# Attention inner loop: the products with V gathered into two blocks per head, six slots of exponentials, maxima dealt 3, 5, 3, 5

## The chip, the cores and the metric

The kernel runs on one core of one Trainium2 chip. The core has five engines that run their own instruction streams and meet only at semaphores: TensorE (PE, whose weight loads are shown apart as PEld), VectorE (DVE), ScalarE (ACT), GpSimd (POOL) and SyncE (SP), which here only issues DMAs. The metric is the device time of one execution in microseconds. Before the change the median of 3 runs is 615.58 us (614.25 to 616.12).

## The reference

The program is one transformer layer on 1024 tokens (32 x 32) of 384 channels in float32: attention with 12 heads of 32 channels and a decomposed relative position bias, then a mixture of 8 experts. The change touches only the attention:

```
q, k, v = split(layernorm(x) @ w_qkv + b_qkv)          # 12 heads, 1024 x 32 each
attn = einsum('bnd,bmd->bnm', q * scale, k)             # 1024 x 1024 per head
attn = attn + rel_h[..., :, None] + rel_w[..., None, :]
attn = softmax(attn, axis=-1)
out  = attn @ v
x = x + out @ w_proj + b_proj
```

All of the expert part follows after that and is the same in both kernels.

## The kernel before, in words

For each head the bias is folded into the product: `qst` and `kst` hold 128 rows (q, its low part and the two bias factors against k and two one-hot rows), so that one 128-deep product gives scores with bias. The scores are made turned, with keys on partitions, so that the exponentials can be used as they are in the product with V.

A head takes these steps, and the work of several heads is interleaved on each engine.

- **Maxima** (PE `max_scores`, L536): for the row maximum, 16 matmuls of 128 x 512 per head make the scores once more with queries on partitions, alternately into PSUM banks 4 and 5. DVE takes the maximum of each (`reduce_max`, L1130). The matmul of piece p waits until the reduction of piece p - 2 is done. These are made one head ahead of the scores.
- **Turning the maxima**: DVE combines the halves (`whole_max`), PE transposes the 128 x 8 result (`turn_max`, L542), DVE negates it into `mneg` (`negate_max`), and SP copies it by DMA into a row of `qst` (`max_row`, L317). The first score matmul of the next head waits for that DMA (`mrow_in`).
- **Scores** (PE `scores`, L550): 8 tiles of 128 keys per head, 4 matmuls of 128 x 512 for each tile (two halves of the queries, two parts of the keys), into banks 0 and 1 for even tiles and 2 and 3 for odd ones. The first matmul of tile t waits until the exponential of tile t - 2 has emptied the banks.
- **Exponentials** (ACT, L924): one instruction of 128 x 1024 per tile, from PSUM into a slot of `prob`. There are 4 slots; a slot is free once PE has used it for V and, for the first 7 tiles, once POOL has added it to the sum.
- **Sum** (POOL `add_probs`, L390 and L394): POOL adds the exponentials of the first 7 tiles of a head into `acc`, 6 instructions of 128 x 1024.
- **Values** (PE `values`, L559): the product with V. `vh` (32 channels) is the stationary operand, and `quarters` spreads the 1024 queries over four column groups of the array, each 32 columns wide, so these matmuls use the array split into four tiles of 128 x 32, where all others use it whole. One call of `values` does a pair of score tiles, which the profile shows as 16 matmul records: four rounds of four that run side by side. With the last pair of a head come two more rounds for the sum of the last tile and two for `acc`.
- **Output** (ACT `copy_output` L929, PE `turn_output` L583, DVE `normalise`): the accumulated bank 6 is copied to `osb`, transposed into bank 7, and divided by the sum.

The order on PE is written out by hand in `head`. A head has four periods i = 0 to 3 of two score tiles each. Before the change each period begins with one call of `values` (pairs 2 and 3 of the head before, then pairs 0 and 1 of its own), followed by four maxima placed among the eight score matmuls: M ssss M ss M ss M (M for a maxima matmul, s for one of the scores). In period 2 `turn_output` follows the values, in period 3 `turn_max`. The four maxima of period 3 are already those of the head after next. The heads 1 to 9 run in a hardware loop of three heads per turn. Head 0 makes its 16 maxima in three periods (5, 5, 6), the last head makes none.

## Time and profile before

| | |
|---|---|
| median of 3 runs | 615.58 us (614.25 to 616.12) |
| the profiled execution, its own time | 615.08 us |
| its span | 613.3 us |
| mean granted TensorE clock | 0.996 |
| attention loop in the trace | about 82 to 289 us |

The page gives for each engine its busy time and what it waited for. A matmul's record lasts from its start to a modelled end, and records overlap, since the next begins before the last has drained; the distance from start to start is what a matmul costs. A row of the timeline gives the start, the time from there to the end of the last instruction merged into it, the engine, the line of the code, the tiles written and read, and the number of instructions. Behind it, in brackets, stands idle time of the engine and what ended it.

### The profile page before, as it was taken

The numbers are of one execution on the slowest core, as the hardware profiler recorded it, in microseconds if no ns is written. First come the engines' busy times: TensorE is split into PE (matmuls) and PEld (weight loads), VectorE is DVE, ScalarE is ACT, GpSimd is POOL, SyncE is SP. The second block draws the span as 40 slices with busy tenths as digits, with TensorE's granted clock in tenths as the row PEclk, the third lists the DMA queues.
The fourth block names the chain that finished last, engine by engine and source line by source line (L and its number), as shares of the span: only waits on it lengthen the run. The fifth ranks groups of instructions, "written<-read, shape, count | busy, mean of one in ns | idle before, by whom it ended". The sixth has DMA issues, their size and how long they took to land.

```text
span 613.3 us, 11388 instructions
## 1 busy us (share of the span) xinstructions
PE 590.4 (96%) x4409; PEld 501.9 (82%) x4409; DVE 386.7 (63%) x644; ACT 297.8 (49%) x411; POOL 195.1 (32%) x114
## 2 busy tenths in 40 slices
PE   2998999999999999999998999999999999999996
PEld 2886876666666666666997999999999999999994
DVE  6557767676767666642789875555476545477535
ACT  3555425454545454455456534444555444355523
POOL 0400047898888888898300000000000000000000
PEclk9999999999999999999989999999999999999999
DMA  8046054332344444102050624444442444542302
GB/s 272 7 87 129 3 117 98 69 64 60 68 86 86 86 86 86 40 2 88 17 192 4 228 84 152 153 154 155 155 152 82 156 154 155 155 155 82 113 1 103
DMA packets 37414, 63.39 MB, mean 103 GB/s; under 512 B 3864, under 2 KB 32894, under 8 KB 37246
## 3 DMA queue, kind: packets, MB, share of 16 engines
q1 hardware_dynamic: 37374, 62.83, 36.3%
q8 instruction: 29, 0.48, 0.3%
q14 instruction: 11, 0.09, 0.0%
HBM read 44.16 MB, written 1.57 MB: 75 GB/s over the span
## 4 chain that ended last, share of the span: by engine, by line
PE 91%; DVE 4%; ACT 1%; DMA 1%; SPq 1%; issue 1%; DVEq 0%
PE ps L767 21%; PE ps L783 21%; PE ps L550 14%; PE ps L559 10%; PE ps L536 8%; PE ps L460 8%; DVE rhalf L1130 2%; PE ps L490 1%; PE ps L445 1%; PE ps L701 1%; PE ps L583 1%; DMA onehot<-c_onehot 1%; PE ps L738 1%; PE ps L794 1%; PE ps L713 1%; DVE xs L1296 1%
## 5 line engine op out<-in xcount | busy, mean ns | idle before, releaser
L1130 DVE TENSOR_REDUCE rhalf<-ps 128x1 f32<-128x512 f32 x192 | 131.2, 690 | 40.7 <-PE ps L536 39.8
L924 ACT ACTIVATE prob<-ps 128x1024 f32<-128x1024 f32 x96 | 98.0, 1026 | 97.0 <-PE ps L550 87.5
L394 POOL TENSOR_TENSOR acc<-acc,prob 128x1024 f32<-128x1024 f32 x58 | 139.6, 2406 | 5.9 <-POOL acc L390 0.8
L550 PE MATMUL ps<-qst,kst 128*128 128x512 f32 x384 | 110.6, 394 | 0.0
L767 PE MATMUL ps<-xeh,wih 128*128 128x320 f32 x288 | 89.6, 311 | 1.0 <-ACT xeh L986 1.0
L421 POOL CAST dpc<-dpt 120x1024 fp32r<-120x1024 f32 (+1 forms) x3 | 3.1, 1037 | 273.4 <-PE ps L803 216.6
L783 PE MATMUL ps<-hh,woh 128*128 128x320 f32 x288 | 89.2, 310 | 0.0
L783 PE MATMUL ps<-hh,wol 128*128 128x320 f32 x288 | 89.0, 309 | 0.0
L767 PE MATMUL ps<-xeh,wil 128*128 128x320 f32 x288 | 89.0, 309 | 0.0
L783 PE MATMUL ps<-hl,woh 128*128 128x320 f32 x288 | 89.0, 309 | 0.0
L767 PE MATMUL ps<-xel,wih 128*128 128x320 f32 x288 | 89.0, 309 | 0.0
L550 PEld LDWEIGHTS ps<-qst,kst 128*128 128x128 f32 x384 | 71.8, 188 | 15.2 <-issue 0.8
L536 PE MATMUL ps<-kst,qst 128*128 128x512 f32 x192 | 80.6, 423 | 2.4 <-DVE rhalf L1130 1.3
L1207 DVE TENSOR_TENSOR wol<-raw_o,woh 128x1152 fp32r<-128x1152 f32 x32 | 43.4, 1356 | 50.8 <-ACT woh L959 50.8
L990 ACT ACTIVATE hh<-ps 128x320 fp32r<-128x320 f32 x96 | 41.7, 439 | 55.8 <-PE ps L767 55.0
L959 ACT ACTIVATE woh<-raw_o 128x1152 fp32r<-128x1152 f32 x32 | 37.4, 1168 | 50.0 <-PE ps L783 50.0
L1202 DVE TENSOR_TENSOR wil<-raw_i,wih 128x1152 fp32r<-128x1152 f32 x32 | 43.4, 1357 | 24.4 <-ACT wih L954 24.4
L1281 DVE SCALAR_TENSOR_TENSOR hl<-ps,hh 128x320 fp32r<-128x320 f32 x96 | 45.9, 488 | 19.9 <-ACT hh L990 17.7
L767 PEld LDWEIGHTS ps<-xeh,wih 128*128 128x128 f32 x288 | 54.1, 188 | 1.2 <-ACT xeh L986 1.2
L767 PEld LDWEIGHTS ps<-xel,wih 128*128 128x128 f32 x288 | 54.1, 188 | 0.0
L783 PEld LDWEIGHTS ps<-hl,woh 128*128 128x128 f32 x288 | 54.1, 188 | 0.0
L783 PEld LDWEIGHTS ps<-hh,woh 128*128 128x128 f32 x288 | 54.1, 188 | 0.0
(159 smaller groups left out, 876.3 us busy)
## 6 DMA issues: line engine op xcount, KB each, us to landing
raw_i<-in_L_ffn_wi SPq DMA_DIRECT2D x32, 576.0 KB, 5.1
raw_o<-in_L_ffn_wo SPq DMA_DIRECT2D x32, 576.0 KB, 4.1
xs<-in_x SPq DMA_DIRECT2D x8, 384.0 KB, 4.7
qst<-qh SPq DMA_DIRECT2D x12, 256.0 KB, 3.2
qst<-relh SPq DMA_DIRECT2D x12, 256.0 KB, 3.8
qst<-relw SPq DMA_DIRECT2D x12, 256.0 KB, 4.4
kst<-kp SPq DMA_DIRECT2D x12, 256.0 KB, 5.0
qst<-ql SPq DMA_DIRECT2D x12, 128.0 KB, 3.1
```

Source lines behind the costliest of these rows:

```text
L394: nc.gpsimd.tensor_tensor(acc[:, :], acc[:, :], prob[:, t % SLOT, :], ALU.add).then_inc(sum_add, 1)
L460: done = mm(out_bank, a, b, start=first and n == 0, stop=last and n == 2)
L536: mm(bank(4 + half), qst[b][:, 0, t * P:(t + 1) * P], kst[b][:, 0, half * BANK:(half + 1) * BANK], start=True, stop=True).then_inc(max_mm, 1)
L550: last = mm(bank(2 * (t % 2) + half), kst[b][:, part, t * P:(t + 1) * P], qst[b][:, part, half * BANK:(half + 1) * BANK], start=part == 0, ...
L559: last = mm(bank(6)[HD * j:HD * (j + 1), cols], stationary, moving[:, j * Q4:(j + 1) * Q4], start=start, stop=stop, skip_group_check=True)
L767: last = mm(bank(k, SLOTS), w[:, b, c, k * P:(k + 1) * P], xe[:, c, e, :], start=c == 0 and n == 0, stop=c == DC - 1 and n == 2)
L783: last = mm(bank(3 + c, SLOTS), w[:, b, k, c * P:(c + 1) * P], h[:, b, k, :], start=s == 0 and k == 0 and n == 0, stop=s == UNITS - 1 and ...
L924: run(prob[:, t % SLOT, :], ps[:, 2 * (t % 2) * BANK:2 * (t % 2 + 1) * BANK], ACT.Exp).then_inc(exp_done, 1)
L1130: ve.tensor_reduce(rhalf[:, p // 2, p % 2:p % 2 + 1], bank(4 + p % 2), AX_X, ALU.max).then_inc(max_red, 1)
L1202: ve.tensor_tensor(wil[:, b, :, :], raw_i[:, b, :, :], wih[:, b, :, :].bitcast(F32), ALU.subtract).then_inc(wi_lo, 1)
L1207: ve.tensor_tensor(wol[:, b, :, :], raw_o[:, b, :, :], woh[:, b, :, :].bitcast(F32), ALU.subtract).then_inc(wo_lo, 1)
L1281: stt(out=hl[:, b, k, :], in0=bank(k, SLOTS), scalar=0.0, in1=hh[:, b, k, :].bitcast(F32), op0=ALU.max, op1=ALU.subtract).then_inc(h_lo, 1)
```

## The change

The change is in the attention loop and has these parts.

- PE: the four pairs of a head are no longer dealt one to each period. Pairs 2 and 3 of the head before (with the sum) stand together ahead of period 1, pairs 0 and 1 together ahead of period 3. Periods 0 and 2 begin with scores.
- PE: the maxima are dealt 3, 5, 3, 5 to the periods, in place of four each. A period of five has the pattern M ss M ss M ss M ss M, one of three ssss M ss M ss M.
- `turn_max` writes into bank 5 (before, bank 7), and the second maxima matmul of the head after next, which also writes bank 5, waits for `mneg_ready`. `turn_output` moves to period 3, directly behind `turn_max`.
- ACT and POOL: `prob` has 6 slots, tile t of head h sits in slot (8 h + t) mod 6. The waits in `free_slot` follow from that. ACT's loop now has three heads per turn.
- DVE: `normalise` of a head comes one head later, ahead of the ninth maximum. Near the end `normalise(NH - 3)` and `normalise(NH - 2)` stand around `attn_low(1)`.
- `mneg` and `bpj` are placed elsewhere in SBUF, to make room.

The core of the diff:

```
-    SLOT = 4
+    SLOT = 6
...
+        def slot_of(j, t):
+            return (NT * j + t) % SLOT
...
+                if p == 1:
+                    wait(pe, mneg_ready, h)
...
             def turn_max(h):
                 pe.wait_ge(max_whole, h + 1)
-                wait(pe, o_normed, h - 1)
-                nc.tensor.transpose(bank(7)[0:NT, 0:P], rmax[:, :], ident[:, :]).then_inc(max_turned, 1)
+                nc.tensor.transpose(bank(5)[0:NT, 0:P], rmax[:, :], ident[:, :]).then_inc(max_turned, 1)
...
+            PIECES = [(5, 8), (8, 13), (13, 16)]
+            NEXT = PIECES[0][0]
...
-                        pieces = [(after, p) for p in range(4)] if more else []
+                        pieces = [(after, p) for p in range(NEXT)] if more else []
...
-                        pieces = [(nxt, p) for p in range(4 * i + 4, 4 * i + 8)]
-                    if i > 1:
-                        values(h, b, i - 2)
-                    elif not first:
-                        values(h - 1, (b - 1) % 3, i + 2)
-                    if i == 2 and not first:
-                        wait(pe, mneg_ready, h + 1)
-                        turn_output(h - 1)
-                    if i == 3 and not last:
-                        turn_max(h + 1)
-                    maxima(pieces[0:1])
+                        pieces = [(nxt, p) for p in range(*PIECES[i])]
+                    if i == 1 and not first:
+                        values(h - 1, (b - 1) % 3, 2)
+                        values(h - 1, (b - 1) % 3, 3)
+                    if i == 3:
+                        values(h, b, 0)
+                        values(h, b, 1)
+                        if last:
+                            pe.wait_ge(o_normed, NH - 2)
+                        else:
+                            turn_max(h + 1)
+                        if not first:
+                            turn_output(h - 1)
+                    ahead = int(len(pieces) > HALF)
+                    maxima(pieces[0:ahead])
                     scores(h, b, 2 * i, 0)
+                    maxima(pieces[ahead:2 * ahead])
                     scores(h, b, 2 * i, 1)
-                    maxima(pieces[1:2])
+                    maxima(pieces[2 * ahead:2 * ahead + 1])
                     scores(h, b, 2 * i + 1, 0)
-                    maxima(pieces[2:3])
+                    maxima(pieces[2 * ahead + 1:2 * ahead + 2])
                     scores(h, b, 2 * i + 1, 1)
-                    maxima(pieces[3:])
+                    maxima(pieces[2 * ahead + 2:])
...
             def free_slot(h, t):
-                if t % 2 == 0:
-                    wait(act, pv_mm, PAIRS_T * h + t // 2 - 1)
-                if t < ADDED - SLOT:
-                    wait(act, sum_add, (ADDED - 1) * h + t - (ADDED - 1 - SLOT))
-                elif t >= SLOT:
-                    wait(act, sum_add, (ADDED - 1) * h + max(1, t - SLOT))
+                then, was = (h, t - SLOT) if t >= SLOT else (h - 1, t + NT - SLOT)
+                if was % 2 == 0:
+                    wait(act, pv_mm, PAIRS_T * then + was // 2 + 1)
+                if was < ADDED:
+                    wait(act, sum_add, (ADDED - 1) * then + max(1, was))
```

How the order moves on PE is shown at head 10, the first behind the loop, where no register instructions stand between. The place is the start of its period 0. L536 makes maxima, L550 scores, L559 values (`vh_101` is V of head 9). Before:

```order
L559 MATMUL ps<-prob,vh_101 32x256 [waits exp_done]
L559 MATMUL ps<-prob,vh_101 32x256 x7
L536 MATMUL ps<-kst_95,qst_92 128x512 [waits max_red]
L550 MATMUL ps<-qst_91,kst_94 128x512 [waits exp_done,mrow_in]
L550 MATMUL ps<-qst_91,kst_94 128x512 x3
L536 MATMUL ps<-kst_95,qst_92 128x512 [waits max_red]
L550 MATMUL ps<-qst_91,kst_94 128x512 [waits exp_done]
L550 MATMUL ps<-qst_91,kst_94 128x512
L536 MATMUL ps<-kst_95,qst_92 128x512 [waits max_red]
L550 MATMUL ps<-qst_91,kst_94 128x512 x2
L536 MATMUL ps<-kst_95,qst_92 128x512 [waits max_red]
L559 MATMUL ps<-prob,vh_101 32x256 [waits exp_done]
```

The same place after the change, where the lines are L557 for scores, L544 for maxima and L566 for values:

```order
L557 MATMUL ps<-qst_90,kst_93 128x512 [waits exp_done,mrow_in]
L557 MATMUL ps<-qst_90,kst_93 128x512 x3
L544 MATMUL ps<-kst_94,qst_91 128x512 [waits max_red]
L557 MATMUL ps<-qst_90,kst_93 128x512 [waits exp_done]
L557 MATMUL ps<-qst_90,kst_93 128x512
L544 MATMUL ps<-kst_94,qst_91 128x512 [waits max_red]
L557 MATMUL ps<-qst_90,kst_93 128x512 x2
L544 MATMUL ps<-kst_94,qst_91 128x512 [waits max_red]
L566 MATMUL ps<-prob,vh_100 32x256 [waits exp_done]
L566 MATMUL ps<-prob,vh_100 32x256 x7
L566 MATMUL ps<-prob,vh_100 32x256 [waits exp_done]
L566 MATMUL ps<-prob,vh_100 32x256 x7
```

The values that opened the period are gone from there, with one maxima matmul, and stand with the next pair at its end. The scores of a head now begin directly behind those of the head before.

The second place is where head 10 ends and head 11 begins, which has no maxima. Before (L542 is `turn_max`):

```order
L542 MATMUL ps<-ident,rmax 8x128 [waits o_normed,max_whole]
L550 MATMUL ps<-qst_91,kst_94 128x512 [waits exp_done]
L550 MATMUL ps<-qst_91,kst_94 128x512 x3
L550 MATMUL ps<-qst_91,kst_94 128x512 [waits exp_done]
L550 MATMUL ps<-qst_91,kst_94 128x512 x3
L559 MATMUL ps<-prob,vh_102 32x256 [waits exp_done]
L559 MATMUL ps<-prob,vh_102 32x256 x7
L550 MATMUL ps<-qst_92,kst_95 128x512 [waits exp_done,mrow_in]
L550 MATMUL ps<-qst_92,kst_95 128x512 x3
L550 MATMUL ps<-qst_92,kst_95 128x512 [waits exp_done]
L550 MATMUL ps<-qst_92,kst_95 128x512 x3
```

After (L549 is `turn_max`, L590 `turn_output`):

```order
L549 MATMUL ps<-ident,rmax 8x128 [waits max_whole]
L590 MATMUL ps<-ident,osb 128x128 [waits o_copied]
L590 MATMUL ps<-ident,osb 128x128 x3
L557 MATMUL ps<-qst_90,kst_93 128x512 [waits exp_done]
L557 MATMUL ps<-qst_90,kst_93 128x512 x3
L557 MATMUL ps<-qst_90,kst_93 128x512 [waits exp_done]
L557 MATMUL ps<-qst_90,kst_93 128x512 x3
L557 MATMUL ps<-qst_91,kst_94 128x512 [waits exp_done,mrow_in]
L557 MATMUL ps<-qst_91,kst_94 128x512 x3
L557 MATMUL ps<-qst_91,kst_94 128x512 [waits exp_done]
L557 MATMUL ps<-qst_91,kst_94 128x512 x3
```

Four tiles of scores, 16 matmuls, now follow one another with nothing between.

## Rows read from the trace of the kernel before

**Rows 1.** The page, busy time of each engine.
```profile
PE 590.4 (96%) x4409; PEld 501.9 (82%) x4409; DVE 386.7 (63%) x644; ACT 297.8 (49%) x411; POOL 195.1 (32%) x114
```

**Rows 2.** Critical chain, 98 to 262 us: start, duration, what.
```profile
102.93 1.86 PE ps L559 x32
...
258.44 1.86 PE ps L559 x32
```

**Rows 3.** Groups by line, 122.2 to 139.4 us.
```profile
L1130 DVE TENSOR_REDUCE rhalf<-ps 128x1 f32<-128x512 f32 x16 | 11.0, 691 | 3.8 <-PE ps L536 3.7
...
L924 ACT ACTIVATE prob<-ps 128x1024 f32<-128x1024 f32 x8 | 8.2, 1025 | 7.4 <-PE ps L550 7.2 <-POOL acc L394 0.3
...
L550 PEld LDWEIGHTS ps<-qst,kst 128*128 128x128 f32 x32 | 6.0, 188 | 1.2
```

**Rows 4.** Timeline of PE, 131.5 to 148.5 us.
```profile
132.74 0.62 PE L550 MATMUL ps<-qst,kst 128*128 128x512 f32 x2
133.20 0.39 PE L536 MATMUL ps<-kst,qst 128*128 128x512 f32 x1
133.52 1.07 PE L559 MATMUL ps<-prob,vh 128*32 128x256 f32 x16
134.52 0.50 PE L536 MATMUL ps<-kst,qst 128*128 128x512 f32 x1
134.85 1.09 PE L550 MATMUL ps<-qst,kst 128*128 128x512 f32 x4
...
137.15 0.40 PE L536 MATMUL ps<-kst,qst 128*128 128x512 f32 x1
...
139.34 0.50 PE L536 MATMUL ps<-kst,qst 128*128 128x512 f32 x1
...
145.86 0.63 PE L550 MATMUL ps<-qst,kst 128*128 128x512 f32 x2
146.32 0.40 PE L536 MATMUL ps<-kst,qst 128*128 128x512 f32 x1
146.65 1.07 PE L559 MATMUL ps<-prob,vh 128*32 128x256 f32 x16
147.71 0.27 PE L542 MATMUL ps<-ident,rmax 128*8 128x128 f32 x1
```

**Rows 5.** Timeline of DVE, 131.5 to 149.5 us.
```profile
147.49 0.17 DVE L1134 TENSOR_REDUCE rmax<-rhalf 128x8 f32<-128x16 f32 x1
```

**Rows 6.** Timeline of PE in head 0, 82 to 98.5 us.
```profile
84.78 0.98 PE L536 MATMUL ps<-kst,qst 128*128 128x512 f32 x2
85.97 0.50 PE L536 MATMUL ps<-kst,qst 128*128 128x512 f32 x1 [0.20 <-DVE rhalf L1130]
```

**Rows 7.** Timeline of ACT, 131.5 to 149.5 us and 260 to 292 us.
```profile
133.47 1.02 ACT L924 ACTIVATE prob<-ps 128x1024 f32<-128x1024 f32 x1 [0.26 <-PE ps L550]
136.14 1.03 ACT L924 ACTIVATE prob<-ps 128x1024 f32<-128x1024 f32 x1 [1.64 <-PE ps L550]
...
146.52 1.02 ACT L924 ACTIVATE prob<-ps 128x1024 f32<-128x1024 f32 x1 [0.21 <-PE ps L550]
...
270.01 1.94 ACT L924 ACTIVATE prob<-ps 128x1024 f32<-128x1024 f32 x2 [1.55 <-PE ps L550]
```

**Rows 8.** Timeline of POOL, 258 to 292 us.
```profile
260.49 2.40 POOL L390 TENSOR_TENSOR acc<-prob 128x1024 f32<-128x1024 f32 x1 [2.21 <-PE ps L559]
263.04 12.49 POOL L394 TENSOR_TENSOR acc<-acc,prob 128x1024 f32<-128x1024 f32 x5
```

**Rows 9.** Waits, 98 to 262 us: total, times, longest.
```profile
ACT prob L924 <- POOL acc L394: 9.5, 6, 1.9
```

**Rows 10.** Timeline of SP from 130 us; DMA share, 131.0 to 133.4 us in 40 slices.
```profile
131.12 0.70 SPq L317 DMA_DIRECT2D qst<-mneg  x1
...
DMA  0000000000000000000000002100000000000000
```

**Rows 11.** Busy time of the engines and granted clock by stretch.
```profile
315.00:325.00 10.00, 8.41 (x54) 7.75 (x53) 8.48 (x44) 4.36 (x6) 0.00 (x0) 0.84 0.22 61
```

More of the change, by code:

```diff
@@ L96, in metaformer_layer @@
     wqkl, wvl = place("wqkl", [P, DC, 2 * D], F32R, u3), place("wvl", [P, DC, D], F32R, v3)
-    SLOT = 4
+    SLOT = 6
     prob = place("prob", [P, SLOT, T], F32, u2)
     acc = place("acc", [P, T], F32, u2 + 4 * SLOT * T)
-    assert 4 * (SLOT + 1) * T <= TD + 4 * DC * 2 * D
     bv = new("bv", [P, D])
-    bpj = new("bpj", [P, D])
+    at[0] = max(at[0], u2 + 4 * (SLOT + 1) * T)
     qh, ql = (new(n, [P, DC, T], F32R) for n in ("qh", "ql"))
@@ L121, in metaformer_layer @@
     vh = [new(f"vh{b}", [P, NT, HD]) for b in range(3)]
-    mneg = new("mneg", [NT, P], F32R)
+    mneg = place("mneg", [NT, P], F32R, o4 + 7 * BANK)
     rl = new("rl", [P, 2, NT // 2])
@@ L128, in metaformer_layer @@
     b6 = place("b6", [2 * DC, P], F32, o4 + 6 * BANK)
+    bpj = new("bpj", [P, D])
     top = at[0]
@@ L384, in head_values, with add_probs @@
                 nc.gpsimd.tensor_copy(vh[b][:, :, :], vt[:, :, bass.ts(h, HD)]).then_inc(vh_ready, 1)
-            def add_probs(h, added=ADDED):
+            def add_probs(h, j, added=ADDED):
                 pool.wait_ge(exp_done, NT * h + 2)
                 wait(pool, pv_mm, PAIRS_T * h)
-                nc.gpsimd.tensor_tensor(acc[:, :], prob[:, 0, :], prob[:, 1, :], ALU.add).then_inc(sum_add, 1)
+                nc.gpsimd.tensor_tensor(acc[:, :], prob[:, slot_of(j, 0), :], prob[:, slot_of(j, 1), :], ALU.add).then_inc(sum_add, 1)
                 for t in range(2, added):
@@ L393, in add_probs @@
                     pool.wait_ge(sum_add, (ADDED - 1) * h + t - 1)
-                    nc.gpsimd.tensor_tensor(acc[:, :], acc[:, :], prob[:, t % SLOT, :], ALU.add).then_inc(sum_add, 1)
+                    nc.gpsimd.tensor_tensor(acc[:, :], acc[:, :], prob[:, slot_of(j, t), :], ALU.add).then_inc(sum_add, 1)
             head_values(0, 0)
@@ L400, in _ @@
             head_values(1, 1)
-            add_probs(0)
+            add_probs(0, 0)
             with pool.Fori(0, (NH - 3) // 3) as i:
@@ L568, in values @@
                 for t in (2 * i, 2 * i + 1):
-                    last = quarters(slice(0, Q4), vh[b][:, t, :], prob[:, t % SLOT, :], t == 0, t == NT - 1)
+                    last = quarters(slice(0, Q4), vh[b][:, t, :], prob[:, slot_of(b, t), :], t == 0, t == NT - 1)
                 if i == PAIRS_T - 2 and h_last:
@@ L572, in values @@
                     for t in range(LAST_ADDED, NT - 1):
-                        last = quarters(slice(Q4, 2 * Q4), ones[:, 0:HD], prob[:, t % SLOT, :], False, False)
+                        last = quarters(slice(Q4, 2 * Q4), ones[:, 0:HD], prob[:, slot_of(b, t), :], False, False)
                 if i == PAIRS_T - 1:
-                    quarters(slice(Q4, 2 * Q4), ones[:, 0:HD], prob[:, (NT - 1) % SLOT, :], False, False)
+                    quarters(slice(Q4, 2 * Q4), ones[:, 0:HD], prob[:, slot_of(b, NT - 1), :], False, False)
                     pe.wait_ge(sum_add, (ADDED - 1) * (h + 1) - (ADDED - LAST_ADDED) * h_last)
@@ L681, in _ @@
             project(0, (0, 1))
+            pe.wait_ge(o_normed, NH - 1)
             turn_output(NH - 1)
@@ L923, in exps @@
                     free_slot(h, t)
-                    run(prob[:, t % SLOT, :], ps[:, 2 * (t % 2) * BANK:2 * (t % 2 + 1) * BANK], ACT.Exp).then_inc(exp_done, 1)
+                    run(prob[:, slot_of(j, t), :], ps[:, 2 * (t % 2) * BANK:2 * (t % 2 + 1) * BANK], ACT.Exp).then_inc(exp_done, 1)
                     between(t)
@@ L934, in attn_high @@
                     run(ath[:, c, half * BANK:(half + 1) * BANK], bank(4 + half), ACT.Copy).then_inc(turn_act, 1)
-            exps(0, lambda t: None)
-            with act.Fori(1, NH - 1) as h:
-                exps(h, lambda t: copy_output(h - 1) if t == 1 else None)
+            exps(0, 0, lambda t: None)
+            with act.Fori(0, (NH - 3) // 3) as i:
+                for j in range(1, 4):
+                    exps(3 * i + j, j % 3, lambda t: copy_output(3 * i + j - 1) if t == 1 else None)
+            exps(NH - 2, (NH - 2) % 3, lambda t: copy_output(NH - 3) if t == 1 else None)
             def last_between(t):
@@ L1150, in normalise, with head @@
                                  rl[:, :, :].unsqueeze(3).broadcast_to([P, 2, HALF, HD]), ALU.mult).then_inc(o_normed, 1)
-            def head(h, first=False, more=True):
-                for p in range(0 if first else 4, 2 * NT):
-                    if p == 12 and not first:
-                        normalise(h - 1)
+            NEXT = 5
+            def head(h, first=False, early=False, more=True):
+                for p in range(0 if first else NEXT, 2 * NT):
+                    if p == 8 and not first and not early:
+                        normalise(h - 2)
                     reduce_max(h + 1, p)
+                if not first and not early:
+                    dve.wait_ge(o_normed, h - 1)
                 whole_max(h + 1)
@@ L1160, in head @@
                 if more:
-                    for p in range(4):
+                    for p in range(NEXT):
                         reduce_max(h + 2, p)
@@ L1174, in _ @@
             head(0, first=True)
-            with dve.Fori(1, NH - 2) as h:
+            head(1, early=True)
+            with dve.Fori(2, NH - 2) as h:
                 head(h)
@@ L1187, in _ @@
             ve.tensor_tensor(wpl[:, :, :], wpj[:, :, :], wph[:, :, :].bitcast(F32), ALU.subtract).then_inc(wp_lo, 1)
+            normalise(NH - 3)
+            attn_low(1)
             normalise(NH - 2)
-            attn_low(1)
             normalise(NH - 1)
```

12 lines of the change are left out of this document (6 added, 6 removed).

## The prediction, on record before the changed kernel ran

> **What bounds the kernel now.** I read the page's busy times first: PE is busy 96% of the span and DVE, the next, 63% [rows 1]. Then the chain of waits over the attention loop: it consists of PE work, and the long values blocks, one per head, give the head's period. The first and the last of ten such blocks start at 102.93 and 258.44 us, so nine heads take 155.51 us, 17.28 us each [rows 2]. In one head DVE reduces for 11.0 us and ACT makes exponentials for 8.2 us [rows 3]; POOL adds for 2.40 + 12.49 us, from 260.49 to 275.53 [rows 8]. All have slack, so in this loop only what lies on PE counts.
>
> Then the timeline of PE, from start to start. Two scores and the maxima matmul behind them go from 145.86 to 146.32, 0.23 us for each [rows 4]. The 48 matmuls of a head thus take about 11.0 of the 17.28 us. A short values block goes from 133.52 to 134.52, and from the maxima matmul ahead of it to the one behind it 1.32 us pass (133.20 to 134.52). For the long block, eight rounds in place of four, it is 2.19 us (137.15 to 139.34) [rows 4]. So a round costs (2.19 - 1.32) / 4 = 0.22 us, and the first matmul behind a block takes 0.33 us to the next (134.52 to 134.85) in place of 0.23. What a block costs beyond its rounds is therefore 1.32 - 4 x 0.22 - 0.23 + 0.10 = 0.32 us (with 0.217 for a round). That is the price of leaving the 128 x 128 form of the array for the 128 x 32 form and coming back, and it is what this change is about.
>
> **The change part by part.**
>
> *Blocks.* Before, head 0 has 2 blocks of values, heads 1 to 10 have 4 each, head 11 has 5 (the last two pairs are one block): 47. After, they are 1, 20 and 3: 24. The rounds stay the same. 23 x 0.32 = -7.4 us, all on PE's path.
>
> *`turn_max`.* It now comes behind two pairs of values. Before, PE waits for DVE there: the combined maximum ends at 147.49 + 0.17 = 147.66 [rows 5] and the transpose starts at 147.71, 1.06 us after its block began, where the unhindered block takes 1.00 [rows 4]. With a block one us longer that wait is gone: 11 x 0.06 = -0.6 us. Its flag reaches PE 0.05 us after DVE's end, which I use below.
>
> *Maxima 3, 5, 3, 5.* The pattern M ss keeps 3 x 0.23 = 0.69 us between maxima, and a reduction takes 0.691 [rows 3]. Five in a row are no tighter than four. In head 0 the maxima are not covered: at the end of a period two stand together and then the next period's one, at 84.78, some 0.5 later and 85.97 [rows 6], the last after idle time on DVE. Three adjacent ones take 85.97 - 84.78 = 1.19 us from the first to the third in place of 0.46, so 0.7 too much. By the order this place and two like it cost about 1.8 us in all (0.7, 0.3 for a pair, 0.7). The new order has three pairs, at 0.3 to 0.4 each, 1.0. So -0.8 us (0 to -1.2).
>
> *Waits of scores for exponentials.* This is the price. Two pairs of banks hold the scores; a block between the periods gave ACT time. Now periods 3 and 0, and 1 and 2, touch. Let x be the start of the last score matmul of a tile. The exponential starts at x + 0.43 if nothing else precedes it (x = 145.86 + 0.23, exponential at 146.52), at x + 0.50 (132.74 + 0.23, 133.47) or at x + 0.59 (134.85 + 3 x 0.23, 136.14) where ACT first passes one or two waits against a register [rows 4, 7]. It takes 1.03, and the flag 0.05. Then PE must load: 0.10 us if only the exposed part counts (the 0.33 against 0.23 behind a block), 0.19 if the whole load does [rows 3]. Of an odd tile (7, 3) the next tile but one should start seven matmuls later, x + 1.61 (one maxima, four scores, one maxima): it can at x + 1.61 to 1.70 for tile 7 and at x + 1.68 to 1.77 for tile 3, going by the waits that ACT's order has there. For the even tiles (6, 2) eight matmuls lie between, x + 1.84 against 1.77 to 1.86. Sum per head 0.07 to 0.27 us; an exponential that starts a little late adds to it. I take 0.2, near the upper end, since the load of a waiting matmul beside a running one shows as 188 ns [rows 3]. Ten heads: +2.0 us (0.7 to 3.4).
>
> The Trainium skill, page "TensorE: Matmul & The Clock Gate", section "LDWEIGHTS (loading the stationary operand)", gives columns / 1.2 in ns, 107 ns for 128 columns. By that rule these waits would cost near their lower end, some 0.7 us, and the sum would be 608.3. The trace has both numbers, 0.10 exposed and 188 ns for a load beside a matmul [rows 3, 4], and no wait of this kind.
>
> *Scores without maxima.* From period 3 of head 10 to period 0 of head 11, and in periods 1 and 2 of head 11, four tiles follow each other without any maxima. There the next tile but one is due five matmuls after x, at 1.15, but the exponential allows 0.43 + 1.03 + 0.05 + 0.10 to 0.19 = 1.61 to 1.70: about 0.5 us. The tile after that is bound to the second of two exponentials, which end 1.94 after the first began [rows 7]: about 0.1. Twice this is +1.3 us (0.8 to 1.7). Before, a block of values covered it.
>
> *What costs nothing, and its cover.* The DMA of the maxima row: SP issues at 131.12, 0.6 us after the transpose, and its packets move at 132.5 [rows 10], 2.0 us after the transpose. The score that needs it comes behind `turn_output` and thirteen matmuls, some 3.6 us after it (before 4.35). SP's queue is otherwise the same. POOL's sum: the chain of one head runs from 0.6 us after the last read of `acc` for 15.0 us [rows 8], and PE wants the result about 16.3 us after that read: 0.7 us of cover. The longer ACT loop and the later `normalise` lie on engines with slack. ACT's waits for slots, 9.5 us in ten heads [rows 9], go away with six slots, but no PE matmul waited at their end, so that gives nothing.
>
> *Sum.* -7.4 - 0.6 - 0.8 + 2.0 + 1.3 = -5.5 us. The profiled execution took 615.08 us, so 609.6; it lies 0.5 below the median of the runs, and between 609.6 and 610.1 I say 609.8.
>
> **The rivals.**
>
> *A. The waits for exponentials don't show.* For it: with the exposed load alone most of them are within 0.1 us of being met. Then -8.8 + 0.7 + 0.8 = -7.3, 607.8, and with waits fully absorbed 606.5. Against: tile 3 is late by either count.
>
> *B. The waits are as large as the gain.* If ACT starts every exponential at x + 0.59 and loads count in full, the odd tiles are late by 0.25 and the even ones by 0.03, and ACT falls behind by 0.1 at each: 0.7 us per head, the worth of two blocks and the turn wait (2 x 0.32 + 0.06). Only head 0 and head 11 remain: 614.5, no change.
>
> *C. Slower: the two pairs of score banks become the bound.* Place: tiles 0, 1, 4 and 5 of each head. It decides from 0.18 us at each of the four places. Each wait delays the next exponential, so that ACT and PE take turns rather than overlap; at 0.3 us each it is +1.2 per head against -0.7, and the kernel takes 615.1 + 5 - 1 = 619. Against it: ACT is idle 7.4 us in each head [rows 3] and catches up in every block.
>
> *D. The adder.* POOL's chain of 15.6 us with the read of `acc` behind it binds only if PE's head gets below 16.2 us. I expect 16.8. In rival A the head takes 16.6 us, so even there it does not bind, and it cannot make the kernel slower; it has no chance of its own here.
>
> *E. The clock.* From 315 to 325 us the mean granted clock is 0.84 [rows 11], that is a stretch of 3.2 us at 1.2 GHz (0.16 x 10 x 2) in the routing, while PE had little to do. Work before it now ends 5 us earlier, and the low stretch may fall on matmuls that count. Half of it, 1.6 us, would be lost at most, and 0.5 won at best.
>
> **How the numbers follow.** The forecast with its own range, 606.9 to 612.3 (every wait at its bounds), has 0.70. A has 0.14. B, with anything between 612.3 and 615, has 0.11. C has 0.04 and E carries 0.01 past the edge. The range 606.5 to 613.6 takes A and E's loss, and a part of B. What a measurement of this kernel can tell from no change is about 0.3%, 1.85 us: faster means below 613.7. That is the forecast, A and a small part of B, 0.85; same 0.11; slower 0.04.
>
> **What would show it.** The chain's long blocks, twelve rounds now, should repeat every 16.8 us (16.5 to 17.0) in place of 17.28. PE's timeline should show two blocks per head, one with values x32 then the sum's 16 records, one with values x32, `turn_max` and `turn_output`, and the same 1.00 us and 0.33 at the edges. Waits of scores for ACT should appear at the first matmul of tiles 1 and 5, 0.0 to 0.3 us each, and about 0.5 us at tile 0 of head 11 and at its tile 4. ACT should no longer wait for POOL. The prediction is wrong if a block of four tiles costs more than 8 x 0.22 + 0.32, if the waits exceed 0.35 us per head, or if PE waits for POOL's sum or for the maxima row.

## The result and the profile after

| | us |
|---|---|
| changed kernel, 4 runs | 608.72 median (608.3 to 610.03) |
| kernel before, 4 runs on the same chip | 615.12 median (614.25 to 616.12) |
| ratio | 0.9895, 95% interval 0.9877 to 0.9914 |
| the changed kernel's profiled execution | 610.03, span 608.2, mean granted clock 0.994 |

The kernel is 1.05% faster, 6.4 us by the medians; 609.8 had been forecast, within 606.5 to 613.6. The profiled execution is the slowest of the four, and the trace says why (below, at the clock).

The chain of waits of the changed kernel, 98 to 270 us (start, duration, what), still consists of PE work. The long blocks, now twelve rounds:

```profile
100.69 2.73 PE ps L566 x48
...
117.26 2.73 PE ps L566 x48
...
133.83 2.73 PE ps L566 x48
...
150.72 2.73 PE ps L566 x48
...
167.32 2.73 PE ps L566 x48
```

They repeat every 16.57 to 16.60 us where it was 17.28 [rows 2], except from 133.83 to 150.72, which is 16.89. I return to that one.

PE's timeline of the same kernel, 131.5 to 150.5 us, is to be read from start to start:

```profile
133.44 0.40 PE L544 MATMUL ps<-kst,qst 128*128 128x512 f32 x1
133.76 1.93 PE L566 MATMUL ps<-prob,vh 128*32 128x256 f32 x32
135.51 0.61 PE L566 MATMUL ps<-prob,ones 128*32 128x256 f32 x8
135.95 0.61 PE L566 MATMUL ps<-acc,ones 128*32 128x256 f32 x8
136.49 0.50 PE L544 MATMUL ps<-kst,qst 128*128 128x512 f32 x1
136.83 0.63 PE L557 MATMUL ps<-qst,kst 128*128 128x512 f32 x2
...
140.53 0.39 PE L544 MATMUL ps<-kst,qst 128*128 128x512 f32 x1
140.75 0.70 PE L557 MATMUL ps<-qst,kst 128*128 128x512 f32 x2
141.30 0.39 PE L544 MATMUL ps<-kst,qst 128*128 128x512 f32 x1
...
142.31 1.93 PE L566 MATMUL ps<-prob,vh 128*32 128x256 f32 x32
144.17 0.27 PE L549 MATMUL ps<-ident,rmax 128*8 128x128 f32 x1
...
147.49 0.40 PE L544 MATMUL ps<-kst,qst 128*128 128x512 f32 x1
147.90 1.20 PE L557 MATMUL ps<-qst,kst 128*128 128x512 f32 x4
148.94 0.40 PE L544 MATMUL ps<-kst,qst 128*128 128x512 f32 x1
```

Three things are to be seen. The price of a block is as before: from the maxima matmul ahead of the long block to the one behind it 3.05 us pass (133.44 to 136.49), and 3.05 - 12 x 0.217 - 0.23 + 0.11 = 0.33 us. The one visible stop of a head is at tile 5: two scores from 140.75 to 141.30, 0.55 in place of 0.46 [rows 4]. And at 147.49, where the loop of three heads turns, PE needs 0.41 us to the next score and 1.04 us for the four scores of the tile, against 0.23 and 0.91 elsewhere: 0.31 us once in three heads.

What was waited for, 98 to 262 us (total, times, longest):

```profile
...
POOL acc L400 <- ACT prob L938: 4.6, 9, 0.8
PEld ps L557 <- ACT prob L938: 4.3, 19, 0.4
```

The 4.3 us in 19 waits are 17 weight loads at tiles 1 and 5 and two directly behind a turn of the loop (0.42 and 0.39 us). At the tiles nearly all of it is time in which PE still worked on the matmul before. ACT's wait for POOL [rows 9] is gone, and nothing on PE waits for the maxima row or for POOL's sum.

To compare runs I cut every trace at four points of PE's timeline: the first maxima matmul behind the values' projection, the first read of `acc`, the tenth read of `acc`, and the first matmul of the output's projection. These give head 0 and most of head 1, nine heads of the loop, and the tail. For the changed kernel the ends are these rows:

```profile
82.34 0.39 PE L544 MATMUL ps<-kst,qst 128*128 128x512 f32 x1
...
102.81 0.61 PE L566 MATMUL ps<-acc,ones 128*32 128x256 f32 x8
...
282.76 0.44 PE L466 MATMUL ps<-wph,ath 128*128 128x384 f32 x1
```

All traces together ("low" is the time at 1.2 GHz behind the attention, without the last 0.7 to 2.3 us of the program, which are at 1.2 GHz in every trace):

| kernel | heads 0-1 | nine heads | tail | attention | from there to the end | low |
|---|---|---|---|---|---|---|
| before | 21.93 | 155.52 | 29.76 | 207.21 | 323.77 | 3.4 |
| changed | 20.47 | 149.85 | 30.10 | 200.42 | 325.38 | 6.8 |
| changed, again | 20.44 | 150.00 | 30.13 | 200.56 | 323.76 | 3.4 |
| four blocks | 21.84 | 154.75 | 29.85 | 206.43 | 324.74 | 3.4 |
| four slots | 20.61 | 149.92 | 30.30 | 200.83 | 323.36 | 0 |
| split blocks | 21.62 | 156.03 | 29.97 | 207.61 | 325.18 | 6.8 |
| maxima 4, 4, 4, 4 | 20.37 | 149.05 | 30.18 | 199.61 | 325.23 | 6.8 |
| maxima between | 20.41 | 149.46 | 30.13 | 199.99 | 323.74 | 3.4 |
| turn at a block | 20.41 | 149.60 | 30.14 | 200.14 | 325.19 | 6.8 |
| three edits | 20.41 | 148.91 | 29.52 | 198.84 | 323.72 | 3.4 |
| three edits, again | 20.42 | 148.94 | 29.49 | 198.85 | 325.19 | 6.8 |
| three edits, 4444 | 20.36 | 148.84 | 29.47 | 198.68 | 325.23 | 6.8 |
| three edits, four slots | 20.57 | 148.98 | 29.69 | 199.25 | 323.78 | 3.4 |

The attention repeats to 0.15 us between executions of one kernel, the rest only to 1.6, and the last column goes with it but for one trace (324.74). So the sum is checked against the attention, where the change is: -6.79 us.

### The profile page after: what moved, and what is told of

Its sections match the earlier page's. It is cut to its first block, busy times and chain, and to the rows that moved or that the text cites. A ratio compares the mean times of both kernels' runs of the same rounds, so it can differ in the third digit from the quotient of the medians.

```text
span 608.2 us, 11363 instructions
## 1 busy us (share of the span) xinstructions
PE 584.4 (96%) x4409; PEld 504.5 (83%) x4409; DVE 387.2 (64%) x644; ACT 297.9 (49%) x411; POOL 195.3 (32%) x114
## 4 chain that ended last, share of the span: by engine, by line
PE 90%; DVE 5%; ACT 2%; DMA 1%; issue 1%; SPq 1%; DVEq 0%
PE ps L782 21%; PE ps L798 21%; PE ps L557 14%; PE ps L566 9%; PE ps L466 8%; PE ps L544 7%; DVE rhalf L1146 2%; PE ps L716 1%; PE ps L496 1%; PE ps L451 1%; DMA onehot<-c_onehot 1%; PE ps L753 1%; PE ps L728 1%; PE ps L809 1%; PE ps L590 1%
## 5 line engine op out<-in xcount | busy, mean ns | idle before, releaser
L557 PE MATMUL ps<-qst,kst 128*128 128x512 f32 x384 | 115.6, 397 | 0.9 <-ACT prob L938 0.9
L557 PEld LDWEIGHTS ps<-qst,kst 128*128 128x128 f32 x384 | 70.0, 188 | 19.2 <-ACT prob L938 5.5
L544 PE MATMUL ps<-kst,qst 128*128 128x512 f32 x192 | 78.4, 412 | 2.0 <-DVE rhalf L1146 0.9
```

Source lines behind the costliest of these rows:

```text
L544: mm(bank(4 + half), qst[b][:, 0, t * P:(t + 1) * P], kst[b][:, 0, half * BANK:(half + 1) * BANK], start=True, stop=True).then_inc(max_mm, 1)
L557: last = mm(bank(2 * (t % 2) + half), kst[b][:, part, t * P:(t + 1) * P], qst[b][:, part, half * BANK:(half + 1) * BANK], start=part == 0, ...
```

## The experiments

My theory: the gain is the number of blocks, 0.32 us each, less small waits of scores for exponentials. Rivals: the gain comes from the other edits (slots, bank, the deal of maxima), or the waits cost as much as foreseen and the blocks are worth more.

**Four blocks.** The changed kernel, with the values and maxima in the order of before:

```diff
-            PIECES = [(5, 8), (8, 13), (13, 16)]
+            PIECES = [(4, 8), (8, 12), (12, 16)]
...
-                    if i == 1 and not first:
-                        values(h - 1, (b - 1) % 3, 2)
-                        values(h - 1, (b - 1) % 3, 3)
+                    if i > 1:
+                        values(h, b, i - 2)
+                    elif not first:
+                        values(h - 1, (b - 1) % 3, i + 2)
...
+                    cut = [pieces[0:1], [], pieces[1:2], pieces[2:3], pieces[3:]]
...
```

> The changed kernel with one part undone: the pairs of values are dealt one to each period again and the maxima 4 to a period in the old pattern (M ssss M ss M ss M); six slots, bank 5 for the turned maxima and turn_output behind turn_max stay. Theory (the gain is the form changes of the array): back to about 614 to 615 us, head period 17.2 us (17.28 less the 0.06 that turn_max no longer waits in a few heads, if that), ACT's waits for POOL gone all the same. Rival (the gain comes from the free slots or from the bank of the turned maxima): stays at 609 to 611.

Measured: 614.14 us (613.71 to 616.12, 10 runs), ratio to before 0.9985 (0.9969 to 1.0001). The attention is 0.78 us shorter than before; a head takes 17.19 us. The bank, the slots, the place of `turn_output` and the later `normalise` are worth 0.8 us together, the regrouping (with its deal of maxima and with the turn wait) 6.0. The turn wait is not in the 0.8, for in this kernel it is still there. PE's timeline, 144.5 to 147.8 us:

```profile
145.54 1.07 PE L566 MATMUL ps<-prob,vh 128*32 128x256 f32 x16
146.60 0.27 PE L549 MATMUL ps<-ident,rmax 128*8 128x128 f32 x1
```

The transpose starts 1.06 us behind its block's start, as before [rows 4], at ten of the eleven places (1.13 at the last), and each time 0.05 us behind the end of DVE's combined maximum. Of the 0.8 us, 0.3 is a delay that the kernel before has in the first head of each turn of the loop: at 113.11, 165.00 and 216.84 us the maxima matmul behind `turn_max` starts 0.19 us after it, in the other heads 0.09. With four blocks it is gone. The rest is 0.05 us a head, of which 0.03 lie where `turn_output` now stands right behind `turn_max`. The cause of the delay was not looked for.

**Four slots.** One number of the changed kernel:

```diff
-    SLOT = 6
+    SLOT = 4
```

> The changed kernel with SLOT = 4. Theory: slots alone gave nothing before, but with blocks of four tiles the exponentials of tiles 0 and 1 cannot start until the block has read their slots, and the scores of tiles 2 and 3 behind the block wait for them: about 1.3 to 1.6 us more at each of two blocks, head period 19 to 20 us, 640 to 650 us in all. Rival (the slots don't matter, ACT has 7 us of idle time in a head): 609.

Measured: 607.57 us (606.44 to 609.6, 4 runs), ratio 0.988 (0.9849 to 0.9912); attention 200.83. I was wrong by over 30 us: the slots are not needed, and in the attention they are worth 0.4 us. ACT's timeline of this kernel, 131 to 138 us, shows it:

```profile
134.30 1.94 ACT L938 ACTIVATE prob<-ps 128x1024 f32<-128x1024 f32 x2 [2.86 <-PE ps L566]
136.12 0.60 ACT L943 ACTIVATE osb<-ps 128x512 f32<-128x512 f32 x1
137.65 1.03 ACT L938 ACTIVATE prob<-ps 128x1024 f32<-128x1024 f32 x1 [0.92 <-PE ps L557]
```

and PE's:

```profile
133.08 1.93 PE L566 MATMUL ps<-prob,vh 128*32 128x256 f32 x32
...
135.81 0.50 PE L544 MATMUL ps<-kst,qst 128*128 128x512 f32 x1
136.15 0.62 PE L557 MATMUL ps<-qst,kst 128*128 128x512 f32 x2
```

A block of two pairs gives back the slots of its first pair after four rounds, so the exponentials of tiles 0 and 1 run from 134.30 to 136.24, beside the rest of the block (the four rounds of its first pair end about 0.9 us behind 133.08). Tile 2 wants the first one's banks at 136.15, when it has been done (at 135.3) for 0.8 us. What I had overlooked is that the two exponentials that wait have a whole block as cover.

**Split blocks.** The changed kernel, with the first maxima matmul of a period moved from behind the block in between its two calls of `values`, so that a head has four blocks again while the scores stand as in the changed kernel:

```diff
-                    for head_max, p in pieces:
+                    for head_max, p in filter(None, pieces):
...
                         values(h - 1, (b - 1) % 3, 2)
+                        maxima(pieces[0:1])
+                        pieces = [None] + pieces[1:] if pieces else []
                         values(h - 1, (b - 1) % 3, 3)
                     if i == 3:
                         values(h, b, 0)
+                        maxima(pieces[0:1])
+                        pieces = [None] + pieces[1:] if pieces else []
                         values(h, b, 1)
```

> The changed kernel with one maxima matmul moved from behind each block into its middle, so that the array changes form twice more per head, 20 more blocks in heads 0 to 10; the matmuls are the same. Theory (0.32 us for each block beyond its rounds): +6.4 us, 615 us, head period 17.2 us. Rival (blocks cost their rounds only, the gain came with what else moved, the dealing of maxima and the turn waits): 609.

Measured: 615.96 us (614.93 to 617.21, 10 runs), ratio 1.0008 (0.9992 to 1.0024). Attention 207.61, +7.19 us against the changed kernel for 20 more blocks: 0.36 us each. In the nine heads alone it is +6.18 us for 18 blocks, 0.34 each. PE's timeline of this kernel, 116 to 136 us:

```profile
117.82 0.39 PE L544 MATMUL ps<-kst,qst 128*128 128x512 f32 x1
118.14 1.07 PE L566 MATMUL ps<-prob,vh 128*32 128x256 f32 x16
119.14 0.49 PE L544 MATMUL ps<-kst,qst 128*128 128x512 f32 x1
119.56 1.07 PE L566 MATMUL ps<-prob,vh 128*32 128x256 f32 x16
120.45 0.61 PE L566 MATMUL ps<-prob,ones 128*32 128x256 f32 x8
120.88 0.61 PE L566 MATMUL ps<-acc,ones 128*32 128x256 f32 x8
121.42 0.73 PE L557 MATMUL ps<-qst,kst 128*128 128x512 f32 x2
```

One single maxima matmul inside the block costs 1.42 us from block start to block start (118.14 to 119.56) where its four rounds take 0.87 and the matmul 0.23: 0.32 us more. The matmuls are the same in both kernels, so this settles that leaving the 128 x 32 form and coming back is what was paid for; what the array does in that time no run shows. The gain of the whole change is undone by it (207.61 against 207.21 us before), so no other part of it carries the gain: the rest comes to nothing on balance.

**Maxima 4, 4, 4, 4.** The changed kernel, with four maxima in each period, one ahead of each two scores (M ss M ss M ss M ss):

```diff
-            PIECES = [(5, 8), (8, 13), (13, 16)]
+            PIECES = [(4, 8), (8, 12), (12, 16)]
...
-                    ahead = int(len(pieces) > HALF)
-                    maxima(pieces[0:ahead])
+                    cut = [pieces[0:1], pieces[1:2], pieces[2:3], pieces[3:4], pieces[4:]]
+                    maxima(cut[0])
                     scores(h, b, 2 * i, 0)
-                    maxima(pieces[ahead:2 * ahead])
+                    maxima(cut[1])
...
```

> The changed kernel with its two blocks, but the maxima dealt 4 to each period as M ss M ss M ss M ss. Theory: the only waits of scores for exponentials in a full head are 0.10 us at tile 5 and 0.0 to 0.03 at tile 1, where four scores stand together; with a maxima matmul between all pairs these tiles start eight matmuls after the tile before and never wait: head period 16.47 in place of 16.57, -1.0 us. Rival (the dealing 3, 5, 3, 5 is itself needed, since DVE cannot take sixteen maxima at 0.69 us without the gaps): PE waits for DVE, 16.6 us or more.

Measured: 608.29 us (606.87 to 609.68, 6 runs), ratio 0.9883 (0.9859 to 0.9908). Attention 199.61, 0.81 us less than with 3, 5, 3, 5. PE's timeline of this kernel, first ahead of a block of values, then where the loop turns (between the scores at 147.24 and the maxima matmul at 147.69):

```profile
133.25 0.40 PE L544 MATMUL ps<-kst,qst 128*128 128x512 f32 x1
133.48 0.62 PE L557 MATMUL ps<-qst,kst 128*128 128x512 f32 x2
134.03 1.93 PE L566 MATMUL ps<-prob,vh 128*32 128x256 f32 x32
...
147.24 0.62 PE L557 MATMUL ps<-qst,kst 128*128 128x512 f32 x2
147.69 0.39 PE L544 MATMUL ps<-kst,qst 128*128 128x512 f32 x1
147.92 0.61 PE L557 MATMUL ps<-qst,kst 128*128 128x512 f32 x2
```

At tiles 1 and 5 hardly a stop is left, the heads take 16.52 to 16.60 us, and the turn's 0.3 us is gone: 147.24 to 147.69 and 147.69 to 147.92 are the pace. A head without a turn still gains only 0.03 of the 0.1 expected. The block's entry is not what takes it back: 0.55 us behind the start of two scores (133.48 to 134.03) is 0.09 more than the pace of 0.46, the same 0.09 as 0.32 against 0.23 behind a maxima matmul. What takes part of it back is the pace itself: the 44 intervals of a head between such matmuls are 231.8 ns in the mean, stops of over 15 ns left out, where they are 230.7 in the changed kernel, 0.05 us a head. Why was not tested. The deal of 3 and 5 is therefore no part of the gain: it costs 0.8 us, most of it at the loop's turns.

**Turn at a block.** The end of PE's loop moved from ahead of period 0 to ahead of period 1:

```diff
-            def head(h, n, b, first=False, last=False, more=True):
+            def head(h, n, b, first=False, last=False, more=True, periods=range(4)):
...
-                for i in range(PAIRS_T):
+                for i in periods:
...
-                    head(3 * i + j, i + j // 3, j % 3)
+                    head(3 * i + j, i + j // 3, j % 3, periods=range(1, 4))
+                    head(3 * i + j + 1, i + (j + 1) // 3, (j + 1) % 3, periods=range(1))
```

> The changed kernel, with the end of the three-head loop moved on every engine: the loop body now holds periods 1, 2, 3 of a head and period 0 of the next, so PE's jump stands just ahead of the block of values of periods 1, not ahead of four scores. Theory (the jump costs about 0.3 us where scores follow it directly, because their weight loads cannot be fetched ahead, and less where a block follows, whose mode change is paid anyway): the two heads with a turn take 16.6 to 16.7 us in place of 16.89 and 16.84, the others stay at 16.57 to 16.60, the loop over nine heads 149.4 in place of 149.85. Rival (the 0.3 us is the maxima or another wait that happens to fall in that head): the turns still take 16.85, or the cost moves to another head whole. Time 608.2 to 608.7 either way.

In this text "on every engine" says too much: only PE's loop is cut differently, the loops of the others are as they were. Measured: 607.73 us (606.93 and 608.52), ratio 0.9874 (0.9847 to 0.9901). All nine heads take 16.59 to 16.66 us: no turn stands out any more, the others are 0.03 longer, and the nine heads take 149.60, -0.25. PE's timeline of this kernel at its turn:

```profile
149.16 0.39 PE L544 MATMUL ps<-kst,qst 128*128 128x512 f32 x1
149.47 1.93 PE L566 MATMUL ps<-prob,vh 128*32 128x256 f32 x32
```

0.31 us from a maxima matmul to a block, as at every other block (0.32). So the 0.3 us belonged to the jump with scores directly behind it; a wait for maxima would have stayed where it was. A block behind the jump hides it, and with 4, 4, 4, 4 a single maxima matmul behind the jump does too. Why the scores pay and the others don't is not shown: the text's reason, that their weight loads cannot be fetched ahead, was not tested.

**Maxima between.** Only the places of the maxima in a period of three changed:

```diff
-                    ahead = int(len(pieces) > HALF)
-                    maxima(pieces[0:ahead])
+                    cut = [pieces[k:k + 1] for k in range(4)] + [pieces[4:]] if len(pieces) > HALF else [[]] + [pieces[k:k + 1] for k in range(3)] + [pieces[3:]]
+                    maxima(cut[0])
                     scores(h, b, 2 * i, 0)
-                    maxima(pieces[ahead:2 * ahead])
+                    maxima(cut[1])
...
```

> The changed kernel, with the maxima inside a period dealt otherwise: a period of three has two scores ahead of each maxima matmul (ss M ss M ss M ss), one of five stays M ss M ss M ss M ss M. Theory (the stop of 0.08 to 0.095 us at tiles 1 and 5 comes from how early the first score of the tile stands behind the previous tile's exponential; two scores later for the maxima changes which tile is early): the head period goes from 16.57 to 16.47 us, the nine heads from 149.85 to about 149. Rival (the head is bound by DVE's reductions of 0.69 us, so an equal pitch moves the stop and doesn't remove it): 16.55 to 16.60. Attention as a whole 199.4 to 200.5 us.

Measured, one run: 606.24 us. A head takes 16.55 us, the turns still 16.82, the nine heads 149.46: -0.39 where I expected about -0.9. The rival's figure was nearer, but not its reason: PE does not stop for DVE. The stops at tiles 1 and 5 are gone, and as with 4, 4, 4, 4 the pace of the other matmuls is 1 ns longer (231.6 ns).

**Three edits.** Both of these and, in the last head, the values by single pairs:

```diff
-                    if i == 1 and not first:
+                    if last and i < 2:
+                        values(h - 1, (b - 1) % 3, i + 2)
+                    elif i == 1 and not first:
...
+                    if last and i == 2:
+                        values(h, b, 0)
                     if i == 3:
-                        values(h, b, 0)
+                        if not last:
+                            values(h, b, 0)
                         values(h, b, 1)
...
```

> Three edits on the changed kernel together: maxima ss M ss M ss M ss in the periods of three, the loop's end ahead of the block of values, and in the last head the values dealt one tile at a time (two blocks more, 0.64 us, against 1.3 us of waits of scores for exponentials, so -0.6). Theory: period 16.47 to 16.55, turns within 0.1 of it, the tail from the last acc read of the loop to the first projection matmul 29.4 to 29.6 in place of 30.10; attention 198.5 in place of 200.42, time 606.7. Rival (the waits of the tail only move to the other blocks): tail 30.1 to 30.7, attention 199.5 to 200.

Measured: 606.82 us (604.5 to 607.61, 5 runs), ratio 0.9856 (0.9832 to 0.9881). Attention 198.84, tail 29.52. The last head of the changed kernel and of this one, from PE's timelines; first the changed:

```profile
261.28 2.07 PE L557 MATMUL ps<-qst,kst 128*128 128x512 f32 x8
263.65 2.08 PE L557 MATMUL ps<-qst,kst 128*128 128x512 f32 x8 [0.30 <-ACT prob L938]
...
269.26 2.11 PE L557 MATMUL ps<-qst,kst 128*128 128x512 f32 x8
271.94 2.12 PE L557 MATMUL ps<-qst,kst 128*128 128x512 f32 x8 [0.57 <-ACT prob L938]
```

and with the three edits:

```profile
259.08 2.09 PE L557 MATMUL ps<-qst,kst 128*128 128x512 f32 x8
261.11 1.07 PE L566 MATMUL ps<-prob,vh 128*32 128x256 f32 x16
262.11 2.11 PE L557 MATMUL ps<-qst,kst 128*128 128x512 f32 x8
```

Eight scores take 8 x 0.23 = 1.84 us; in the changed kernel the next eight follow 2.37 and 2.68 us behind, 0.53 and 0.84 late. A single block in between costs its own 0.32 and covers that. The tail is 0.58 shorter; 0.6 had been expected.

**Three edits with 4, 4, 4, 4.**

> As the kernel with all three edits, but with four maxima in each period (M ss, four times) in place of three and five: period 16.52 to 16.60 as measured for four and four alone, no cost at the turn, the tail 29.4 to 29.6: attention 199.0 us, time 607.0 to 607.5. If the deal of the maxima matters for the waits, this one and the one with three and five differ by over 0.05 us per head; if only the number of blocks does, they are equal.

Measured: 607.74 us (607.54 to 608.86, 4 runs), ratio 0.9873 (0.9854 to 0.9893); attention 198.68, nine heads 148.84 against 148.91. By the rule in the text the two are equal, so the deal no longer matters once the turn and the place of the maxima are right. Their medians are 0.9 us apart; in the traces the difference lies behind the attention (323.72 and 325.23 us).

**Side by side.** The changed kernel, the three edits, and the three edits with four slots, on one chip:

> The changed kernel once more, as the yardstick for the two others of this call: 608.3 to 608.9 us by the runs so far, attention 200.4 us in the trace.

> The kernel with three edits on the changed one (maxima of the periods of three behind two scores each, loop's end ahead of a block, the last head's values one tile pair at a time), once more beside the changed kernel. Theory: the attention stretch is 1.5 us shorter again (198.8 to 200.4) and the medians differ by as much, 606.9 against 608.5. Rival: the gain is given back behind the attention, where the granted clock falls for a stretch or two of 3.4 us whenever work moves, so the medians differ by under 0.8 us.

> The same with four slots of exponentials in place of six. Theory, from the run of the changed kernel with four slots (loop 149.92 against 149.85): the slots give nothing, so attention 198.8 to 199.3 us and the same median as with six. Rival: the tighter order leaves ACT too little room with four slots, attention over 200 us.

Measured: 609.2 us (608.22 to 611.42), 607.74 (606.71 to 608.1) and 607.78 (606.46 to 609.24), 6 runs each; before 615.63. The attention takes 200.56, 198.85 and 199.25 us. The three edits beat the changed kernel by 1.7 us in the attention and 1.5 by the medians, and the traces of the pair even have the low stretches the other way round. The intervals of their ratios to before, 0.9867 (0.9838 to 0.9896) and 0.9898 (0.9867 to 0.993), overlap, so by time alone the difference is likely rather than sure; in the trace it has now repeated. The medians also compare unlike executions: all six of the three edits had a mean granted clock of 0.993, of the changed kernel's only two, and these two took 611.42 and 609.76 us against 606.71 to 608.1. Of the expectations the first missed (609.2 against 608.3 to 608.9), the second has the difference right, and the third has the slots right: 0.4 us, no more, the same as without the three edits.

## Why the prediction was right, point by point

**Blocks, -7.4.** Right. The price of 0.32 us was read from two blocks [rows 4]; the split costs 0.36 each over 20 blocks, 0.34 over the 18 of the nine heads, 0.32 in the rows of one.

**`turn_max`, -0.6.** Right, by the rows. In the changed kernel the transpose starts 1.86 us behind its block's start (142.31 to 144.17), which is eight rounds and the 0.12 that an unhindered block shows too (1.00 against 0.87), and DVE's combined maximum ended at 143.31, 0.86 us earlier. The experiment with four blocks does not show it, since the wait is still in it.

**Maxima in head 0, -0.8.** Right in size, wrong in its name. Heads 0 and 1 take 1.46 us less, of which two blocks are 0.64. With four blocks they gain 0.09, with 4, 4, 4, 4 they gain 1.56. So the 0.8 comes, as far as these orders part it, from the place between the first tile's two pairs of scores, which was empty before and in the kernel with four blocks, and is used with 3, 5, 3, 5 and with 4, 4, 4, 4. The deal 3, 5, 3, 5 itself, which I had costed at nothing in the loop, costs 0.8: 149.85 against 149.05 us.

**Waits of scores for exponentials, +2.0 (0.7 to 3.4).** Right in mechanism, too large; the lower end was near. In the loads of weights of the changed kernel, 140.2 to 141.6 us, tile 5 is seen:

```profile
140.30 0.19 PEld L544 LDWEIGHTS ps<-kst,qst 128*128 128x128 f32 x1
140.72 0.30 PEld L557 LDWEIGHTS ps<-qst,kst 128*128 128x128 f32 x2 [0.24 <-ACT prob L938]
141.06 0.19 PEld L544 LDWEIGHTS ps<-kst,qst 128*128 128x128 f32 x1
```

The load waits until 140.72, 0.19 us after it could start (140.53), the matmul still begins at 140.75, on its pace, and the tile loses 0.09 in all. At tile 1 the load is late too (132.17, with the matmul ahead of it at 132.03), and the pair takes 0.49 us in place of 0.46 (132.25 to 132.74).

So about 0.1 us of lateness costs nothing, and the record's 188 ns do not count in full. The row of two loads hides why: the second starts at 140.83, 0.11 us behind the first, although the first one's record runs to 140.91. A load that has been waited for thus takes 0.11 us, and 140.83 + 0.23 is 141.06, where the second score starts. Per head the stops are 0.11 us, where I took 0.2: +1.1 for ten heads. The step that was mis-sized is the choice near the upper end "since the load of a waiting matmul beside a running one shows as 188 ns". By the Trainium skill, page "TensorE: Matmul & The Clock Gate", section "LDWEIGHTS (loading the stationary operand)", a load takes columns / 1.2 in ns, 107 ns for 128 columns. The trace agrees: 0.11 us from load to load, and a stop of 0.09 behind a load 0.19 late.

The heads without a turn agree with the sum of the terms. Two blocks at 0.32, the turn wait and 0.11 of waits give -0.59; they went from 17.19 us with four blocks, where the other edits are already in, to 16.59, -0.60 (from 17.25 before, -0.66).

**Scores without maxima, +1.3.** Right: 0.53 and 0.84 in the last head, and the tail grew by 0.34 although it has three blocks fewer (-0.96).

**The loop's turn.** Not foreseen: +0.3 at each of two turns in the stretch of nine heads, +0.6 in all. It was missed because I looked at the order at head 10, behind the loop, where no jump stands. Before, the turn cost nothing: the longer heads there (17.36, 17.40 and 17.31 us against 17.25) are those with the delay of 0.10 behind `turn_max`, which the change removed, -0.3.

**Covers.** Right in that POOL's sum, the maxima row and the waits for slots bind nothing (the waits above). POOL's cover is thinner than the 0.7 us foreseen, though: its last addition ends 0.36 to 1.19 us ahead of the read of `acc` in heads 1 to 10, and 0.21 ahead in head 11. Rival D stays out at 16.5 us per head.

**The whole.** Forecast -5.5 us, measured -6.79 in the attention. The difference is the waits (-0.9), the turns (+0.6), the delays behind `turn_max` (-0.3) and what else the other edits gain (-0.05 a head, -0.5); 0.2 stay unassigned. With blocks at 0.34 in place of 0.32 the 0.2 is more than used up, so the price of a block is no better known than that. That the total came out within 1.3 us is in part luck, since terms that nobody foresaw cancel. Rival A (607.8, 606.5 with nothing left of the waits) was half right: the waits show, at half the size. B and C are refuted by the head's 16.57 us. The forecast of 609.8 against 608.72 is 1.1 off, less than the 1.6 us by which the same code behind the attention differs between two executions of the changed kernel.

**E, the clock.** From 300 us on the changed kernel's profiled execution is at 1.2 GHz for 6.8 us on end, twice the 3.4 of before [rows 11]. The stretch from 300 to 310 us, with the busy time and the number of instructions of PE, PEld, DVE, ACT and POOL, then the granted clock, the DMA share and GB/s; the changed kernel:

```profile
300.00:310.00 10.00, 10.00 (x78) 9.88 (x78) 8.19 (x23) 7.64 (x13) 0.00 (x0) 0.86 0.86 262
```

and the kernel with four slots:

```profile
300.00:310.00 10.00, 10.00 (x89) 9.88 (x89) 8.88 (x33) 8.44 (x14) 0.00 (x0) 1.00 0.86 280
```

The first has 2.8 of the ten us from 300 to 310 at 1.2 GHz (0.14 x 10 x 2) and works on 78 matmuls, the second has all ten at 2.4 GHz and works on 89; in both PE was busy all of the time. The 1.6 us that E gave as its loss is what separates the two profiled executions of the changed kernel (325.38 and 323.76 us behind the attention, 610.03 and 608.64 in all). It does not follow the change. The changed kernel and the three edits have both shown 3.4 us in one trace and 6.8 in another, and of the 32 executions of the kernel before on one chip, the eight with a mean granted clock of 0.998 took 614.1 to 615.32 us and the eight with 0.993 took 615.67 to 617.13, 1.9 us more in the mean. What decides it in an execution is open, and no experiment was made on it.

## What to carry to other kernels

Where PE is busy all the time, count how often it changes the form of its array and price one change from start to start, not from busy time. Grouping is worth that price times the number, until a consumer's buffers run out; the waits that come in its place show first as late weight loads, of which the first 0.1 us was free here. Leave the blocks apart only where nothing else fills the gap (the last head), keep the loop's jump from standing right ahead of a tile of scores, and try each "needed" buffer by itself: two of the six slots gave 0.4 us of the 6.8. An experiment that takes one part back should be looked at for the other terms too: with four blocks the turn wait came back as well.

## What was not expected of the hardware

- The turn of PE's loop costs 0.31 and 0.26 us where a tile of scores follows it, and nothing that can be seen where a block of the other array form follows (0.31 against 0.32 us) or a maxima matmul (0.45 us for the two scores ahead of it, with 4, 4, 4, 4).
- A weight load recorded as 186 ns that begins 0.03 us ahead of its matmul's start (140.72, 140.75) does not delay that start in the record; the stop shows one matmul later, and the next load starts 0.11 us behind it.
- The time behind the attention, the same code in all thirteen traces, varies from 323.36 to 325.38 us, and with it the time at 1.2 GHz from 0 to 6.8 us (in one trace, at 324.74 us with 3.4, the two don't go together).
